# Four of sixteen top-value masks on GpSimd, and counts verified by ScalarE in one pass

## The reference

```python
z = x_flat @ ternary_quant(W_syn).T + b_syn          # 2048 tokens x 1024 hidden values
k = max(1, int(N * (1.0 - TARGET_SPARSITY)))         # 102
topv, _ = jax.lax.top_k(z, k)
thresh = topv[:, -1:]                                # the 102nd largest of each token
hidden = jnp.where(z >= thresh, jax.nn.relu(z), 0.0)
out = hidden @ ternary_quant(W_out).T + b_out
out = layernorm(x + out, gamma, beta)
```

## Time and profile before

| | us |
|---|---|
| median of 3 runs | 859.98 |
| lowest to highest | 858.42 to 862.5 |
| profiled execution, its own time | 861.84 |
| its span in the trace | 860.2 |
| VectorE busy over the span | 537.5 (62%) |
| GpSimd busy over the span | 467.9 (54%) |
| ScalarE busy over the span | 270.8 (31%) |
| TensorE matmul busy over the span | 636.0 (74%) |

### The profile page before, as it was taken

How to read it: one execution, slowest core, us unless ns; L and a number is a source line. 1 busy time by engine, 2 the same in 40 slices (tenths; PEclk the granted TensorE clock), 3 DMA queues, 4 the chain that set the end, 5 groups by cost and what they waited for, 6 DMA issues and landing times.

```text
span 860.2 us, 12191 instructions
## 1 busy us (share of the span) xinstructions
PE 636.0 (74%) x2938; PEld 480.4 (56%) x2938; DVE 537.5 (62%) x1717; ACT 270.8 (31%) x591; POOL 467.9 (54%) x503
## 2 busy tenths in 40 slices
PE   1378996000398867887999647999999999999940
PEld 1244552000287754565666535888788888888720
DVE  3778885999778877897888443344354453443522
ACT  1113343869423320233333312223233232232200
POOL 4448786564022220366666660567667667676662
PEclk9579999555599998999899777999999999999985
DMA  7334557786000217354452525799999999999587
GB/s 270 138 112 168 183 195 272 291 337 248 1 19 25 90 27 253 114 181 167 138 172 95 187 105 175 208 219 255 249 237 255 230 257 245 234 256 245 75 179 233
DMA packets 84833, 157.77 MB, mean 183 GB/s; under 512 B 10688, under 2 KB 55168, under 8 KB 84800
## 3 DMA queue, kind: packets, MB, share of 16 engines
q1 hardware_dynamic: 54144, 103.23, 36.2%
q0 software_dynamic: 29792, 53.25, 26.3%
q10 hardware_dynamic: 864, 0.93, 0.3%
HBM read 88.66 MB, written 68.70 MB: 183 GB/s over the span
## 4 chain that ended last, share of the span: by engine, by line
PE 54%; DVE 19%; issue 9%; DMA 5%; ACT 5%; another core or an unknown queue 3%; POOL 2%; DVEq 1%; SPq 1%; ACTq 1%; POOLq 0%
PE psum L963 12%; PE psum L756 7%; PE psum L976 6%; PE psum L967 6%; PE psum L981 4%; PE psum L951 4%; PE psum L796 3%; PE psum L894 2%; DMA acc<-hh,toki 2%; DVE qT L1366 2%; PE psum L738 2%; PE psum L728 1%; DVE hh L1474 1%; PE psum L828 1%
## 5 line engine op out<-in xcount | busy, mean ns | idle before, releaser
L689 POOL DMA_INDIRECT acc<-hh,toki x128 | 199.2, 1556 | 97.3 <-DVE hh L1747 56.8
L1747 DVE TENSOR_SCALAR hh<-psum,wtok 128x256 f32<-128x256 f32 x128 | 56.0, 480 | 158.0 <-DMA acc<-hh,toki 79.4
L652 POOL DMA_INDIRECT xs_rows<-Z,slot x96 | 99.9, 1040 | 50.9 <-issue 27.4
L963 PE MATMUL psum<-qT,Z 128*128 128x256 f32 x512 | 121.4, 380 | 1.2 <-DVE hh L1737 0.8
L963 PEld LDWEIGHTS psum<-qT,Z 128*128 128x128 f32 x512 | 92.3, 190 | 11.8 <-issue 1.9
L578 POOL TENSOR_TENSOR rstd<-mv,neghalf 128x1 f32<-128x1 f32 (+1 forms) x48 | 30.7, 640 | 108.3 <-DVE mv L1238 108.3
L1172 ACT ACTIVATE qT<-psum 128x512 f32<-128x512 f32 x64 | 38.1, 597 | 103.5 <-PE psum L951 101.6
L756 PE MATMUL psum<-wt,hTs 128*128 128x512 f32 x128 | 61.3, 623 | 12.6 <-ACT hTs L1057 7.7
L967 PE MATMUL psum<-qT,Z 128*112 128x256 f32 x256 | 65.7, 379 | 0.0
L976 PE MATMUL psum<-Z,hh 128*128 128x256 f32 x256 | 60.6, 379 | 1.2 <-DVE hh L1737 1.2
L779 PE MATMUL psum<-bad,onesf 128*128 128x1 f32 x2 | 0.6, 348 | 79.5 <-DVE bad L1426 79.5
(11 more groups left out here) (288 smaller groups left out, 1344.9 us busy)
## 6 DMA issues: line engine op xcount, KB each, us to landing
Z<-in_wexp SPq DMA_DIRECT2D x66, 496.0 KB
xs_rows<-fill POOLq DMA_DIRECT2D x64, 272.0 KB, 2.8
Z<-xs_rows SPq DMA_DIRECT2D x64, 272.0 KB
Z<-kv_rows SPq DMA_DIRECT2D x16, 688.0 KB
kv_rows<-Z SPq DMA_DIRECT2D x12, 688.0 KB, 3.8
acc<-fill POOLq DMA_DIRECT2D x4, 1024.0 KB, 8.5
ctxH_s<-in_ctxH SPq DMA_DIRECT2D x16, 224.0 KB, 3.9
wt<-in_wd SPq DMA_DIRECT2D x66, 48.0 KB
```

The source lines that it names most:

```text
L652: pool.indirect_dma_start(out=xs_rows[:, :], out_offset=bass.IndirectOffsetOnAxis(ap=slot[:, t, k:k + 1], axis=0), in_=H[:, t, :], in_offs ...
L689: pool.indirect_dma_start(out=acc[s % 2][:, :], out_offset=bass.IndirectOffsetOnAxis(ap=toki[:, g, j:j + 1], axis=0), in_=y_sb[:, s, j, :] ...
L963: m = pe.matmul(pA[par][:, g * CAP:(g + 1) * CAP], wgu_sb[:, s, k, g * P:(g + 1) * P], xT[:, par, k, :], start=(k == 0), stop=(k == 1))
L1747: m = dve.tensor_scalar(y_sb[:, s, j, :], pY[par][:, j * D:(j + 1) * D], wtok[:, g, j:j + 1], None, ALU.mult)
```

## The change

Three things change.

1. GpSimd makes masks 3, 7, 11 and 15, each by two instructions, a compare (`tensor_scalar`, 1024 values) and a multiplication (`tensor_tensor`), into slot 3 of `hh`. VectorE makes the other twelve. The 64 fills are split: 16 stand ahead of the masks, 48 behind them.
2. ScalarE counts in one pass of 16 instructions: Sign of 2^64 (thr - z) with its sum. This gives +1 below the point, -1 above it and 0 at it, so the count comes as half integers when a value equals the point.
3. The comparison for the masks is "at or below" in place of "below", so a value equal to the point comes out as the first maximum. `counts` (ahead of max 14) and `verdict` (behind max 15) take the place of the old `verdict`; a token with a value equal to its point now goes to the exact branch.

```diff
--- before.py
+++ after.py
@@ -255,7 +255,7 @@
         cnt_done = sem("cnt_done")
         masked = sem("masked")
         max_done = sem("max_done")
-        above_done = sem("above_done")
+        pool_masked = sem("pool_masked")
         below_done = sem("below_done")
         bad_ready = sem("bad_ready")
         bad_done = sem("bad_done")
@@ -627,9 +627,20 @@
             pool.iota(fill[:, :, CT:CT + 1], pattern=[[P, 2], [0, 1]], base=T, channel_multiplier=1,
                       allow_small_or_imprecise_dtypes=True).then_inc(c_done, 1)
             pool.wait_ge(c_done, 1)
-            with pool.Fori(0, E) as i:
-                pool.dma_start(rows_v[i, 0:CAP, :].rearrange("(p b) d -> p (b d)", b=2),
-                               fill[:, :, :].rearrange("p b d -> p (b d)")).then_inc(filled, 16)
+            def fill_rows(first, last):
+                with pool.Fori(first, last) as i:
+                    pool.dma_start(rows_v[i, 0:CAP, :].rearrange("(p b) d -> p (b d)", b=2),
+                                   fill[:, :, :].rearrange("p b d -> p (b d)")).then_inc(filled, 16)
+
+            fill_rows(0, E // 4)
+            pool.wait_ge(thr_ready, ROUNDS + 1)
+            for t in range(3, NT, 4):
+                if t >= 4:
+                    pool.wait_ge(max_done, t - 3)
+                pool.tensor_scalar(hh[:, 3, :], z[:, t, :], thr[:, t:t + 1], None, ALU.is_le).then_inc(pool_masked, 1)
+                pool.wait_ge(pool_masked, t // 2)
+                pool.tensor_tensor(hh[:, 3, :], hh[:, 3, :], z[:, t, :], ALU.mult).then_inc(pool_masked, 1)
+            fill_rows(E // 4, E)
 
             def norms(b, par):
                 if there(b):
@@ -1089,17 +1100,13 @@
 
 
             act.wait_ge(thr_ready, ROUNDS + 1)
-            for half in range(2):
-                first, end = half * NTD, half * NTD + NTD
-                if half:
-                    act.wait_ge(below_done, first)
-                with act.Fori(first, end) as t:
-                    act.activation(junk[:, t - first, :], z[:, t, :], ACT.Relu, bias=hib[:, bass.ds(t, 1)],
-                                   scale=-BIG).then_inc(above_done, 1)
-                act.wait_ge(above_done, end)
-                with act.Fori(first, end) as t:
-                    act.activation(junk[:, t - first, :], junk[:, t - first, :], ACT.Sign,
-                                   accum_out=below[:, bass.ds(t, 1)]).then_inc(below_done, 1)
+            with act.Fori(0, NTD) as t:
+                act.activation(junk[:, t, :], z[:, t, :], ACT.Sign, bias=hib[:, bass.ds(t, 1)], scale=-BIG,
+                               accum_out=below[:, bass.ds(t, 1)]).then_inc(below_done, 1)
+            act.wait_ge(below_done, NTD)
+            with act.Fori(NTD, NT) as t:
+                act.activation(junk[:, t - NTD, :], z[:, t, :], ACT.Sign, bias=hib[:, bass.ds(t, 1)], scale=-BIG,
+                               accum_out=below[:, bass.ds(t, 1)]).then_inc(below_done, 1)
 
             def evac_hidden(b, par):
                 act.wait_ge(hidT_full, b + 1)
@@ -1412,29 +1419,40 @@
             def mask_tile(t):
                 if t >= 4:
                     dve.wait_ge(max_done, t - 3)
-                dve.scalar_tensor_tensor(hh[:, t % 4, :], z[:, t, :], thr[:, t:t + 1], z[:, t, :],
-                                         ALU.is_lt, ALU.mult).then_inc(masked, 1)
-
-            def verdict():
+                return dve.scalar_tensor_tensor(hh[:, t % 4, :], z[:, t, :], thr[:, t:t + 1], z[:, t, :],
+                                                ALU.is_le, ALU.mult)
+
+            def counts():
 
                 dve.wait_ge(below_done, NT)
-                link(dve.tensor_scalar(chi[:, :], below[:, :], -1.0, float(N), ALU.mult, ALU.add))
+                link(dve.tensor_scalar(chi[:, :], below[:, :], -0.5, N / 2.0, ALU.mult, ALU.add))
                 dve.tensor_scalar(t1[:, :], chi[:, :], -1.0, float(TOPK), ALU.mult, ALU.add)
                 link(dve.tensor_scalar(t2[:, :], chi[:, :], float(NEAR), None, ALU.is_ge))
                 link(dve.scalar_tensor_tensor(t2[:, :], chi[:, :], float(TOPK), t2[:, :], ALU.is_le, ALU.mult))
+
+            def verdict():
+
+                link(dve.tensor_tensor(t3[:, :], m9[:, :, 1], m9[:, :, 0], ALU.is_equal))
+                link(dve.tensor_tensor(t2[:, :], t2[:, :], t3[:, :], ALU.subtract))
                 link(dve.tensor_reduce(bad[:, :], t2[:, :], AX.X, ALU.min))
                 dve.tensor_scalar(bad[:, :], bad[:, :], -1.0, 1.0, ALU.mult, ALU.add).then_inc(bad_ready, 1)
 
-            mask_tile(0)
+            by_dve = 1
+            mask_tile(0).then_inc(masked, 1)
             for t in range(NT):
-                if t + 1 < NT:
-                    mask_tile(t + 1)
+                if t + 1 < NT and (t + 1) % 4 != 3:
+                    mask_tile(t + 1).then_inc(masked, 1)
                 if t == NT - 2:
-                    verdict()
-                dve.wait_ge(masked, t + 1)
+                    counts()
+                if t % 4 == 3:
+                    dve.wait_ge(pool_masked, t // 2 + 1)
+                else:
+                    dve.wait_ge(masked, by_dve)
+                    by_dve += 1
                 alone(dve, "dve")
                 dve.max(m9[:, t, 1:9], hh[:, t % 4, :]).then_inc(max_done, 1)
             dve.wait_ge(max_done, NT)
+            verdict()
             link(dve.tensor_tensor(m9s[:, :, :], iota9[:, None, :].to_broadcast([P, NT, 9]), t1[:, :, None].to_broadcast([P, NT, 9]), ALU.is_equal))
             link(dve.tensor_tensor(m9s[:, :, :], m9s[:, :, :], m9[:, :, :], ALU.mult))
             link(dve.tensor_reduce(thr[:, :], m9s[:, :, :], AX.X, ALU.add))
```

## The result

| | before | after |
|---|---|---|
| median, us | 858.96 (5 runs) | 878.73 (5 runs) |
| lowest to highest | 855.69 to 862.5 | 875.02 to 1769.37 |
| ratio | | 1.0216, 95% interval 1.018 to 1.0253 |

The ratios leave out the slow executions: the profiled one of the changed kernel at 1769 us, with matmuls about twice as long throughout, one of the kernel before at 3708 us (in experiments 9 to 12), and the slowest of experiments 2 and 11 (859.83 and 859.52 us).

The account below looks back on a forecast made before the run. VectorE alone was taken to bound the mask stage. A 17.2 us later add2(0) plus 1.3 us for TensorE's clock made +18.5 us, 878.5 against the median of 859.98; forecast 879 us, range 873.5 to 885.5.

Parts of the forecast that it names:

- VectorE bounds the mask stage, GpSimd is free behind it: Mask stage: VectorE busy 38.5 of 39 us; GpSimd idle for 31.4 us after its last fill, until the first pow.
- ScalarE is worth 0.3 us: Mask stage: one counting pass ends near 206.5 in place of 222.6, but only VectorE's 0.28 us wait was on the path.
- GpSimd's masks: Mask stage: compare 1.3 us, 0.24 us wait, multiplication 2.33 us; the fourth mask ends at 219.5 us.
- The exclusion: Mask stage: a two-input VectorE mask and a GpSimd operation exclude each other whole; a max excludes nothing; 0.2 us waits per repeat.
- VectorE gains 3.7 us: End of mask stage: with four masks fewer, the second stage's first mask starts at 225.3 us, 3.7 us earlier.
- The 48 fills, 39.9 us and 0.5 to enter: GpSimd's queue behind its fourth mask: fills end at 259.9, pow(0) ready at 260.5; add2(0) waits 21 us, starts 17.2 late.
- TensorE's clock, +1.3: Second stage after the wait: TensorE idles 20 us and restarts at half clock, costing 1.3 us, with 0 and 1.8 as ends.
- All later stages follow, nothing is given back: After add2(0): VectorE works through a block in 5 us without slack, so the whole delay stays in the total.
- the rival in which a part is given back: Second stage or convolution absorbs some 5 us of the stall: 873 to 874 us; chance 0.05.
- The multiplication did not get in ahead of mask 2: Rival, mask stage: compare plus gap under 1.14 us, so mask 2 waits 2.2 us: +4.7, 883.5 us; chance 0.08.
- The stall was not hidden: Rival, GpSimd's queue: the 48 fills end near 239, at a pitch of 0.40 us, leaving only the gain: 856 us; chance 0.03.
- The exact branch did not run: Rival: a token with a value equal to its point triggers the exact branch, 480 us and more, about 1360; chance 0.03.

Follow-up runs that it names:

- experiments 9 to 12: In order: the changed kernel unaltered; it with 150 extra multiplications on TensorE during the wait (1.0593); SP issuing all fills, with GpSimd's masks, then without.
- experiment 9: The changed kernel again, no edit, as base for a run on the same chip: ratio 1.0185 (1.014 to 1.023).
- 12: The kernel before with all 64 fills issued by SP, no masks on GpSimd, on the same chip as 11: ratio 0.9964 (0.9936 to 0.9992), median 849.91 us.
- 2: The changed kernel with 40 fills ahead of GpSimd's masks and 24 behind, in place of 16 and 48: ratio 0.9974 (0.9945 to 1.0003).
- 11: The changed kernel with all fills issued by SP, once more on another chip: ratio 0.9914 (0.9886 to 0.9943), median 848.21 us.
- experiment 6: The changed kernel with all sixteen masks on VectorE and all fills in one loop ahead; ScalarE's single pass and new verdict left: ratio 1.0000 (0.9975 to 1.0024).
- experiment 4: The kernel before, all masks on VectorE, but GpSimd issues 16 fills, waits for thr_ready 5 and max 11, then issues 48: ratio 1.0138 (1.0104 to 1.0173).
- 1: The changed kernel again, no edit, for a profile of an undisturbed execution: ratio 1.0172 (1.0137 to 1.0207), own time 871.32 us.
- experiment 3: The changed kernel with all 64 fills issued by SP and none by GpSimd: ratio 0.9907 (0.9883 to 0.9931), 847.68 us beside 854.8.

## Why the prediction was right, point by point

- *VectorE bounds the mask stage, GpSimd is free behind it.* Right.
- *ScalarE is worth 0.3 us.* Right in that it is nearly nothing: experiment 6 measured no change (1.0000).
- *GpSimd's masks.* The term that was mis-sized. I took 1.3 us for the compare; it is 2.85 us alone, and 2.65 to 2.7 beside VectorE once it has begun. It lies above 2.3 us, which the prediction named as a sign that it is wrong, and above my dearest bound, the 2.33 us of the two-input row, which I took to cover any one-input operation. (That row is an addition, line 713, and not a multiplication as I read it; the multiplication measured the same, 2.34.) The exclusion was half right: as assumed, a VectorE mask holds up the start of a compare and a running multiplication holds up a mask; but a compare under way does not. That these two errors nearly cancel is luck: the repeat is 8.54 us (208.68 - 200.14) where 8.32 was forecast, and the fourth mask ends 33.3 us behind hib, forecast 32.2. The Trainium skill's one-input rule ("GPSIMD Engine Reference", "Engine selection": roughly line rate) does not hold for this compare, at 2.85 us for 1024 values beside VectorE's 1.27 us for its whole mask.
- *VectorE gains 3.7 us.* It gained 1.5. The four masks save 4.7 us as forecast. Of that, the three masks that meet a multiplication of GpSimd (drawn 1.65 to 1.72 us) take back 1.3, where 0.8 of waits was forecast; the four operations behind max 15 take 0.7 (0.85 forecast); and the stretch with `counts` takes 2.4 us in place of 1.4, where 0.8 was forecast. The last is the larger part of what was missing: its first operation meets the fourth multiplication and is held for 1.6 us. The prediction's rule knew only VectorE operations with two inputs; this one has one. No row of VectorE shows a wait for GpSimd's result in the mask stage. And only 0.9 of the 1.5 us reached add2(0), since TensorE projected block 0 in 4.19 us in place of 3.62.
- *The 48 fills, 39.9 us and 0.5 to enter.* Measured 38.6 us (223.39 to 261.95) and nothing to enter: the first six were issued without the gap of 0.3 us, the others slightly slower (0.843 against 0.831). add2(0) waits 17.25 us, where 21 was said, because it was reached later, and starts 16.4 us late, forecast 17.2.
- *TensorE's clock, +1.3.* The waiting of residual(3) is 1.82 us (1.44 in experiment 9), where 1.3 was forecast and 1.8 was my upper end, and add2(2) is 1.9 us later than the stall explains (11.65 us behind add2(0), before 9.72). A further 1.5 us is lost before the first pow of the routing stage, which comes 178.6 us behind hib in place of 158.8: +19.9 us in all, forecast 18.5; in experiment 9 it comes 177.2 us behind hib, +18.4.
- *All later stages follow, nothing is given back.* Neither shown nor refuted. The three comparisons of the changed kernel give 1.0216, 1.0172 and 1.0185, which are 18.5, 14.7 and 15.8 us, and the delay alone (experiment 4) costs 11.8 us in all where its first pow of the routing stage comes 16.4 us late. The totals of 1, 4 and 9 thus lie 2.6 to 5.2 us below their paths, and 1 and 9 (873.7 and 874.9 us by their ratios) near the 873 to 874 us of the rival in which a part is given back, to which I gave 0.05. Against runs on the same chip it is mixed: 1 beside 2 loses 21.0 us up to that pow and 18.3 us in the medians, 9 beside 12 loses 18.9 and 21.0. That the first comparison (878.73 us) hit the forecast of 878.5 so closely is in part luck.
- *The rivals.* The multiplication did not get in ahead of mask 2, and no mask waited 2.2 us for it: compare and gap are 2.9 us alone, far above the 1.14. The stall was not hidden: the pitch of a fill was 0.843 us with the transfers at another time. The DMA queues can hardly set it, as they took more from SP: 334 GB/s at 0.86 of the DMA engines' time under GpSimd's fills (256 to 260 us), 367 GB/s at 0.95 under SP's in experiment 3 (180 to 184 us), one each 0.765 us. Even at that pitch 48 fills are 37 us. The exact branch did not run: its rows are in no profile.

## What to carry to other kernels

An instruction queue is a shared resource even when its engine looks idle: ask of every block of work that is moved on it what stands directly behind, and when that is wanted. Here 40 us of DMA issue were hidden, and became a wait of 17 us ahead of a 0.6 us operation. Where DMAs need nothing of their engine, issue them from one whose queue is idle at that time; this version, with the same masks, was 0.9% faster than the kernel before in both comparisons, for reasons that are in part open. And measure a new kind of operation alone before it goes on a path, with a row of the same kind: a two-input operation was no upper bound for a compare.

## What the runs showed of the hardware

- GpSimd's compare of 1024 float32 values with a per-partition point takes 2.85 us, longer than its multiplication of two such tiles, 2.34 us.
- GpSimd's multiplication holds up a VectorE operation with two SBUF inputs (1.65 to 1.72 us in place of 1.26) and a VectorE `tensor_scalar` with one (128x16, 1.78 us in place of 0.16), but not a max (two in 2.35 us beside it at 194.99, as before). GpSimd's compare under way does not hold up a mask (1.26 us).
- Directly behind GpSimd's last multiplication the first six DMA issues of its loop came 0.55 us apart and the others 0.843 (experiments 1 and 2); behind a wait for a semaphore (experiment 4) they came 0.84 to 0.85 us apart from the first. Why was not looked into.
- How long TensorE stays at half clock after a restart differs between executions: from 230.4 to within the window of 232 to 234 before, from 229.2 to past 234 in experiment 3, and the same pair again in 12 and 11. A restart 1.7 us earlier there left 0.6 us (3) and 0.3 us (11) at the first pow or add2(0).
